# An early-fusion block on one core: small transposes on TensorE, 128-row tiles in the text feed-forward, four row buffers, and another order of gathers

## The chip, the cores and the metric

The kernel runs on one NeuronCore of a Trainium2 chip. The metric is the device time of one launch in microseconds (us); smaller is better. The engines are named as in the profile: PE is TensorE (PEld its weight loads), DVE is VectorE, ACT is ScalarE, POOL is GpSimd, SP is SyncE, which issues most DMAs.

## The reference, cut to what matters

There are 32 samples, each of 36 image patches and 77 text tokens, width 256; with a class token a sample has S = 114 rows. All is float32.

```python
h = patches @ tok_W + tok_b                      # 36 rows, with the class token in front
x = layer_norm(emb[tokens] + pos_emb)            # 77 rows
Q, K, V = x @ Wq + bq, x @ Wk + bk, x @ Wv + bv  # 16 heads of 64
logits = Q @ K.T / 8 + causal + where(tokens == 0, -1e9, 0)
x = x + layer_norm(softmax(logits) @ V @ Wo + bo)
x = x + gelu(layer_norm(x) @ W1 + b1) @ W2 + b2  # text feed-forward, 1024 hidden
h = concatenate([h, x], axis=1)                  # 114 rows
h = h + gated_delta_net(layernorm(h))            # convolution, recurrence over the rows, gate
h = h + experts(layernorm(h))                    # top 4 of 32, and a shared one
h = h + state_mixer(layernorm(h))                # convolution, softplus step sizes, 16 states
h = h + factorised_mlp(layernorm(h))             # entmax gates
```

## The kernel before, in words

The program is a row of stages. Each builds its instruction streams, one per engine, inside a block; at its end all engines meet at a barrier, and SP clears the stage's semaphores (`Core.stage`) before the next begins. The order in each stream is written out by hand. The class `Chain` makes VectorE wait for its own instruction where the next one reads what it wrote.

`opening` (L114) takes the image patches through their projection (9 tiles of 128 rows, `image_tokens`, L536) and the text through embedding, norm and attention. Its loads all go through SP's queue in the order of the code: the tokens, a second copy of them to DRAM in another order (L192, one element at a time), patch weights and first patches, position and norm rows, more patches, then behind a wait for that copy the token numbers of all samples broadcast to 77 partitions (`keys`, L205), then the weights of queries, keys and values, the value bias laid out one value per partition (L216, one element at a time), the class token, and then the stores of normalised text rows (`store_text`, L184) and image rows. The normalised rows of a text sample lie in one of two buffers, so `affine(2)` (L292) waits until the store of sample 0 has landed. TensorE does three patch tiles, turns sample 0, and so on to patch tile 8, and then the first products of queries and keys (L463). VectorE turns the token numbers into float and into the mask (L350 to L352).

`text_mlp` (L576) works on 2464 text rows in 11 units of two tiles of 112 rows. Per unit TensorE projects the attended rows with `w_o` (L760), turns the normalised rows (L769), multiplies by `w1` (L783, 224 columns moving) and by `w2` (L797, 256 columns moving). All engines first wait for ten loads under one semaphore `mw_in`. The products of unit m + 2 with `w_o` stand behind unit m's with `w1`.

`prepare` (L834, first part of `delta_net`) reads all rows again in 8 groups of 4 samples, normalises them, stores them turned, and computes two gates per head (L945). A group's rows [114, 4, 256] are loaded by one DMA into one of two buffers (L828); the load of group g + 2 waits for the scaling of group g. VectorE's order is statistics of g + 1, scaling of g, reading of the gates of g - 1.

`delta_net` itself, `route` and `experts` follow; none of them is changed. `state_mixer` (L2162) works on the same 8 groups. GpSimd fetches the experts' rows by indirect DMAs, 16 per group, into one of two buffers (`gather`, L2216), and raises the variances to the power -1/2 (`power`). The order is: group 0, then for each n half of group n + 1, `power(n)`, the other half. VectorE adds the fetched rows times their gates to the residual (`add_routed`, L2243), takes statistics and scales (`norm`); `step_sizes` (L2278) reads the projected step sizes, waits for ScalarE's logarithm (`softplus`) and writes the scaled inputs of TensorE's `turn_bc`. In step j it adds and normalises the groups in `AHEAD`: group 2 in step 0, groups 3 and 4 in step 1, group j + 3 afterwards; `result(j)` then adds the step's output.

## Time and profile before

| | us |
|---|---|
| median of 3 runs (lowest, highest) | 3156.9 (3155.66, 3166.07) |
| the profiled execution | 3159.19 |
| its span, first to last instruction | 3157.5 |
| TensorE, VectorE, ScalarE, GpSimd busy | 2447.2, 2088.9, 1247.4, 809.4 |
| mean granted clock of TensorE | 0.877 |

The stages' places in the span can be read from their first and last instructions: the opening ends near 521 us, the text stage runs from 523.9 to about 771, prepare from 773.7 to 864, the delta stage from 865.8 to about 2150, routing and experts to 2571, the state mixer from 2575 to 2951.5, and the last stage to the end. A busy engine in one of them says nothing about another, so each is read alone. The clock is the share of full speed that TensorE was granted: 1.00 is 2.4 GHz, 0.50 is 1.2 GHz.

### The profile page before, as it was taken

The page shows a single profiled execution, that of the slowest core. Times are in us where ns is not written, and L with a number is a line of the kernel's source. Part 1 is how long each engine was busy: PE and PEld are TensorE (multiplying, and loading weights), DVE is VectorE, ACT ScalarE, POOL GpSimd, SP SyncE. Part 2 cuts the span into 40 slices and gives each one's busy share as a digit, 9 for nine tenths or more (in the row PEclk, how much of TensorE's full clock was granted, in tenths as well). Part 3 has the DMA queues.
Part 4 walks back from the last instruction along what each step waited for, and adds up shares of the span by engine and source line. Part 5 has one row for each costly group of instructions (what it writes and reads, how often), then busy time and mean ns, then how long its engine had stood idle before and what let it go on. Part 6 is the DMA issues. An engine that isn't in the chain of part 4 may idle for free. (4 is left out here: it accounts for less than half of the span.)

```text
span 3157.5 us, 53822 instructions
## 1 busy us (share of the span) xinstructions
PE 2447.2 (78%) x19384; PEld 1877.8 (59%) x19384; DVE 2088.9 (66%) x5024; ACT 1247.4 (40%) x2999; POOL 809.4 (26%) x646
## 2 busy tenths in 40 slices
PE   6888886997455888888888888876543756689798
PEld 5666664886444666666667666655332644466554
DVE  4777773332338888888888888875454336687573
ACT  0434342221145666665666666643000213344132
POOL 1111100000113332233222222231287125550110
PEclk9999997998578999999999999988665887889799
DMA  5220001001212221111112211111211762110000
GB/s 138 64 67 12 12 9 52 21 24 29 87 64 51 52 52 46 49 48 49 44 48 49 51 49 48 45 44 29 74 51 24 227 198 56 47 52 10 18 24 24
DMA packets 277730, 168.94 MB, mean 54 GB/s; under 512 B 186303, under 2 KB 253702, under 8 KB 277112
## 3 DMA queue, kind: packets, MB, share of 16 engines
q1 hardware_dynamic: 251333, 140.22, 15.8%
q0 software_dynamic: 26112, 25.03, 3.0%
q8 instruction: 166, 2.72, 0.4%
q14 instruction: 119, 0.97, 0.1%
HBM read 99.17 MB, written 73.45 MB: 55 GB/s over the span
## 5 line engine op out<-in xcount | busy, mean ns | idle before, releaser
L1149 POOL TENSOR_TENSOR qd<-decay,qm 114x456 f32<-114x456 f32 x128 | 143.7, 1145 | 651.2 <-DVE qm L1242 499.2
L1563 PE MATMUL d_ps<-d_xT,w_qkv 128*128 128x228 f32 x1024 | 235.0, 389 | 48.3 <-DVE qmask L1357 28.9
L1563 PEld LDWEIGHTS d_ps<-d_xT,w_qkv 128*128 128x128 f32 x1024 | 215.4, 212 | 79.5 <-issue 42.0
L2216 POOL DMA_INDIRECT s_eo<-rows_y,slots_all x128 | 152.5, 1191 | 148.5 <-POOLq L87 110.5
L1210 DVE TENSOR_TENSOR elim_tmp<-ue 128x30 f32<-128x30 f32 (+14 forms) x480 | 179.3, 374 | 13.8
L463 PE MATMUL t_ps<-xT,w_qk 128*128 128x154 f32 x1024 | 150.9, 300 | 40.4 <-DVE qk L300 31.0
L1212 DVE TENSOR_TENSOR ue<-ue,elim_tmp 128x30 f32<-128x30 f32 (+14 forms) x480 | 170.4, 355 | 16.5
L1284 DVE SCALAR_TENSOR_TENSOR y_v<-raw,taps,y_v 128x228 f32<-128x228 f32 x384 | 161.2, 493 | 14.3 <-ACT y_v L1414 14.2
L463 PEld LDWEIGHTS t_ps<-xT,w_qk 128*128 128x128 f32 x1024 | 136.7, 189 | 52.0 <-DVE qk L300 38.2
L1551 PE MATMUL d_ps<-gl,after 114*114 114x456 f32 x256 | 132.7, 637 | 41.0 <-DVE sz L1297 41.0
L1376 ACT ACTIVATE decay<-d_ps,gates 114x114 f32<-114x114 f32 x512 | 133.4, 371 | 65.4 <-PE d_ps L1551 65.0
L1809 POOL DMA_INDIRECT rows_x<-r_xn,slot x128 | 144.7, 1131 | 51.9 <-issue 51.0
L1284 DVE SCALAR_TENSOR_TENSOR y_qk<-raw,taps,y_qk 128x228 f32<-128x228 f32 x384 | 142.2, 450 | 22.1 <-ACT y_qk L1414 21.7
L1387 ACT ACTIVATE gl<-upto,gates 114x114 f32<-114x114 f32 x512 | 151.5, 414 | 0.0
L1168 POOL TENSOR_SCALAR_AFFINE_SELECT ue<-ue 128x1024 f32<-128x1024 f32 x16 | 88.8, 5552 | 236.8 <-DMA ue<-blocks_n 236.8
L1596 PE MATMUL d_ps<-w_out,oT 128*114 128x256 f32 x512 | 132.0, 416 | 16.4 <-ACT oT L1433 16.4
L1662 PE MATMUL d_ps<-upd,ut 114*50 114x64 f32 (+1 forms) x2048 | 134.7, 231 | 2.8 <-issue 2.2
L1662 PEld LDWEIGHTS d_ps<-upd,ut 114*50 114x50 f32 (+1 forms) x2048 | 130.9, 142 | 3.8 <-issue 3.1
L1596 PEld LDWEIGHTS d_ps<-w_out,oT 128*114 128x114 f32 x512 | 99.3, 197 | 48.2 <-ACT oT L1433 20.6
L1579 PE MATMUL d_ps<-w_z,d_xz 128*114 128x512 f32 x256 | 117.1, 601 | 10.2 <-DVE sz L1273 9.2
L268 POOL TENSOR_TENSOR rstd<-rstd,minus_half 77x1 f32<-77x1 f32 x32 | 23.5, 734 | 387.9 <-DVE rstd L283 387.9
L405 ACT COPY pT<-t_ps 77x462 f32<-77x462 f32 (+1 forms) x96 | 45.0, 498 | 192.4 <-PE t_ps L513 187.9
(337 smaller groups left out, 5656.9 us busy)
## 6 DMA issues: line engine op xcount, KB each, us to landing
rows_x<-zero_row SPq DMA_DIRECT2D x4, 2048.0 KB, 7.8
ue<-blocks_n SPq DMA_DIRECT2D x16, 512.0 KB, 4.7
blocks_u<-ue SPq DMA_DIRECT2D x16, 512.0 KB, 2.7
blocks_v<-on SPq DMA_DIRECT2D x16, 512.0 KB, 2.8
e_x<-rows_x SPq DMA_DIRECT2D x32, 256.0 KB, 4.2
e_gu<-L_ffn_w_gate_up SPq DMA_DIRECT2D x32, 256.0 KB, 4.2
rows_y<-e_y SPq DMA_DIRECT2D x32, 256.0 KB, 3.3
blocks_n<-nt SPq DMA_DIRECT2D x96, 64.0 KB
```

Source lines behind the costliest of these rows:

```text
L463: last = pe.matmul(ps[:, 6 + f % 3 % 2, (t - lo) * P2:(t - lo + 1) * P2], w_qk[:, k, t * 128:(t + 1) * 128], xT[pair % 3][:, k, :], start= ...
L1149: pool.tensor_tensor(qd[p.par][s][:, hs(u), :].rearrange("p (a o b) t -> p a o b t", o=2, b=2)[:, :, o], e[o][:, :, :].rearrange("p (a b) ...
L1210: ch(dve.tensor_tensor(part, ue[:, j, j + 1:].unsqueeze(1).to_broadcast([128, j, BW - 1 - j]), ue[:, 0:j, j:j + 1].to_broadcast([128, j, B ...
L1212: step = dve.tensor_tensor(ue[:, 0:j, j + 1:], ue[:, 0:j, j + 1:], part, ALU.subtract)
L1284: dve.scalar_tensor_tensor(y, raw[:, t, :, k:k + S], taps[:, t, k:k + 1], y, ALU.mult, ALU.add).then_inc(conv_r, 1)
L1376: last = act.activation(e[o][:, m, :], ps[0:S, 4 + o, m * S:(m + 1) * S], ACT.Exp, bias=gates[:, bass.ds(p.sample(s), 1), head:head + 1].r ...
L1387: last = act.activation(gl[o][:, m, :], c.upto[:, :], ACT.Copy, scale=gates[:, bass.ds(p.sample(s), 1), head:head + 1].rearrange("p a h -> ...
L1563: last = pe.matmul(ps[:, f % 2, (t % 2) * W:(t % 2 + 1) * W], w_qkv[:, k, t * 128:(t + 1) * 128], xT[:, k, :], start=(k == 0), stop=(k == ...
L1596: last = pe.matmul(ps[0:S, 6, 0:D], oT[:, k, :], w_out[:, k, :], start=(k == 0), stop=(k == 7))
L1662: last = pe.matmul(ps[rows, XBANK[m], i * DH:(i + 1) * DH], ut[s][:, 8 * g + i, rows], x[s][:, 8 * g + i, :], start=True, stop=True)
L1809: pool.indirect_dma_start(out=rows_x, out_offset=bass.IndirectOffsetOnAxis(ap=slot[g % 3][:, s, k:k + 1], axis=0), in_=xn[g % 3][:, s, :], ...
L2216: pool.indirect_dma_start(out=eo[n % 2][:, s * TOPK + k, :], out_offset=None, in_=rows_y, in_offset=bass.IndirectOffsetOnAxis(ap=slots_all ...
```

## The change

In the opening, the token numbers as floats are transposed by TensorE into [32, 77], copied from PSUM and stored to DRAM in 32 long rows (the DRAM tensor is now float32); the broadcast of all token numbers comes behind the query and key weights. The value bias is loaded as 8 rows of 128 and transposed by TensorE. The class token's store moves behind the image rows. The broadcast token numbers lie in a buffer `kw` that outlives the stage, and the output weights `Wo` are loaded into it once the mask is made. The mask is computed from it without a cast. TensorE's first patch products wait for the patch weights only, and not for the bias.

In the text stage tiles have 128 rows; the last unit has 128 + 32, and a function `tile` gives each tile's own count to products, transposes and DMAs. The loads are in three semaphores: three norm rows; the rest with `w1`; `w2`. TensorE starts without a wait. Rows of a unit come in two DMAs.

Prepare has four row buffers; the small weights are issued between the load of group 0 and those of 1 to 3; VectorE reads the gates of group g - 2.

In the state mixer GpSimd issues whole groups behind each power from group 2 on: gathers 0, half of 1, power 0, other half of 1, all of 2, power 1, 3, power 2, 4, power 3, and then power n, gathers n + 1. The first group has one semaphore per sample and is added sample by sample (`add_first`). `step_sizes` is cut in two; its second part `step_gates` comes behind the adding of the next group. In step 1 the result is added between groups 3 and 4. ScalarE's `softplus(0)` comes ahead of its read of group 1.

```diff
@@ opening, SP
-                with nc.allow_non_contiguous_dma(reason="2464 token numbers, once"):
-                    sp.dma_start(c.tok_flat.rearrange("(b t) -> t b", b=B), dr["tokens"]).then_inc(flat_in, 16)
...
+                sp.dma_start(bv8[:, :], dr["L0_txt_bv"].rearrange("(k p) -> k p", p=128)).then_inc(bv_in, 16)
                 load_patches(1)
                 load_patches(2)
-                sp.wait_ge(flat_in, 16)
-                sp.dma_start(keys[:, :, :].rearrange("p b t -> p (b t)"), c.tok_flat.partition_broadcast(NT)).then_inc(key_in, 16)
-                sp.dma_start(causal[:, :], dr["causal"]).then_inc(key_in, 16)
+                sp.wait_ge(tokT_ready, 1)
+                sp.dma_start(c.tok_flat.rearrange("(b t) -> b t", b=B), tokT[:, :]).then_inc(flat_in, 16)
...
+                sp.wait_ge(flat_in, 16)
+                sp.dma_start(keys[:, :, :].rearrange("p b t -> p (b t)"), c.tok_flat.partition_broadcast(NT)).then_inc(key_in, 16)
+                sp.dma_start(causal[:, :], dr["causal"]).then_inc(key_in, 16)
                 sp.dma_start(w_v[:, :, :], dr["L0_txt_Wv"].rearrange("(k p) n -> p k n", p=128)).then_inc(wv_in, 16)
-                with nc.allow_non_contiguous_dma(reason="1024 bias values, one per partition and head pair"):
-                    sp.dma_start(b_v[:, :], dr["L0_txt_bv"].rearrange("(k p) -> p k", p=128)).then_inc(wv_in, 16)
...
+                    if i == 20:
+                        sp.wait_ge(mask_ready, 1)
+                        sp.dma_start(kw[:, 0:8 * D].rearrange("p (k n) -> p k n", k=8),
+                                     dr["L0_txt_Wo"].rearrange("(k p) n -> p k n", p=128)).then_inc(wo_in, 16)
@@ opening, TensorE
-                pe.wait_ge(imgw_in, 32)
+                pe.wait_ge(selected, 4)
+                pe.wait_ge(tokf_ready, 1)
+                pe.transpose(ps[0:B, 0, 0:NT], tokf[:, :], c.ident[0:NT, 0:NT]).then_inc(small_mm, 1)
+                pe.wait_ge(imgw_in, 16)
+                pe.wait_ge(tokT_ready, 1)
@@ text_mlp
-    TP = 112
+    TP = 128
     U = 2 * TP
-    UNITS = B * NT // U
+    UNITS = -(-B * NT // U)
+
+    def tile(m, u):
+
+        return min(TP, B * NT - m * U - u * TP)
...
-                pe.wait_ge(mw_in, 16 * MW)
                 project(0)
                 project(1)
                 turn(0)
                 for m in range(UNITS):
                     pe.wait_ge(xT_ready, 2 * m + 2)
+                    if m == 0:
+                        pe.wait_ge(m1_in, 16 * M1)
@@ prepare
+    HB = 4
...
                 load(0)
-                load(1)
                 for dst, src in (
...
+                for g in range(1, HB):
+                    load(g)
                 for g in range(GROUPS):
-                    if g + 2 < GROUPS:
+                    if g + HB < GROUPS:
                         sp.wait_ge(gxn_ready, g + 1)
-                        load(g + 2)
+                        load(g + HB)
...
-                    if g >= 1:
-                        gate_read(g - 1)
+                    if g >= 2:
+                        gate_read(g - 2)
@@ state_mixer, GpSimd
-                for n in range(G):
-                    if n + 1 < G:
-                        gather(n + 1, 0, GS // 2)
+                gather(1, 0, GS // 2)
+                power(0)
+                gather(1, GS // 2, GS)
+                gather(2, 0, GS)
+                power(1)
+                gather(3, 0, GS)
+                power(2)
+                gather(4, 0, GS)
+                power(3)
+                for n in range(4, G):
                     power(n)
                     if n + 1 < G:
-                        gather(n + 1, GS // 2, GS)
+                        gather(n + 1, 0, GS)
@@ state_mixer, VectorE
+                def add_first():
+
+                    for s in range(GS):
+                        dve.wait_ge(s_first[s], 16 * TOPK)
+                        for k in range(TOPK):
+                            ch(dve.scalar_tensor_tensor(c.resid[:, 1 + s, :], eo[0][:, s * TOPK + k, :], gates_all[:, s, k:k + 1],
+                                                        c.resid[:, 1 + s, :], ALU.mult, ALU.add))
+                    dve.sem_inc(s_used, 1)
...
-                    for n in AHEAD.get(j, (j + 3,)):
-                        if n < G:
-                            add_routed(n)
-                            norm(n)
+                    ahead = [n for n in AHEAD.get(j, (j + 3,)) if n < G]
+                    for n in ahead[:1]:
+                        add_routed(n)
+                    if j + 1 < G:
+                        step_gates(j + 1)
+                    for n in ahead[:1]:
+                        norm(n)
                     result(j)
+                    for n in ahead[1:]:
+                        add_routed(n)
+                        norm(n)
@@ state_mixer, ScalarE
                 token_read(0)
+                softplus(0)
                 xT_read(1)
                 first_tap(1)
-                softplus(0)
```

## Rows read from the trace of the kernel before

**Rows 1.** Busy time by stretches: us and instructions per engine, TensorE's granted clock, DMA share, GB/s.

```profile
5.00:12.00 7.00, 0.00 (x0) 0.00 (x0) 0.00 (x0) 0.00 (x0) 1.12 (x2) 1.00 0.44 29
...
523.00:538.00 15.00, 0.00 (x0) 0.00 (x0) 0.00 (x0) 0.00 (x0) 0.00 (x0) 0.50 0.84 262
557.00:771.00 214.00, 209.09 (x1032) 183.20 (x1032) 73.93 (x200) 45.79 (x110) 15.50 (x20) 1.00 0.07 21
787.00:856.00 69.00, 38.00 (x192) 36.75 (x192) 23.56 (x98) 8.85 (x10) 7.27 (x6) 0.50 0.27 95
883.00:1500.00 617.00, 494.11 (x4865) 386.33 (x4867) 507.67 (x1120) 369.89 (x968) 188.60 (x105) 0.90 0.18 45
```

**Rows 2.** Opening in order of time: start, us, engine, line, operation, [idle before].

```profile
1.31 0.99 SPq L192 DMA_DIRECT2D tok_flat<-tokens  x1
...
4.56 7.37 SPq L188 DMA_DIRECT2D attended_t<-patches  x1
...
21.90 10.83 PE L536 MATMUL t_ps<-attended_t 128*128 128x256 f32 x36 [21.90 <-DMA attended_t<-L_tok_b]
...
26.05 4.43 SPq L216 DMA_DIRECT2D b_v<-L_txt_bv  x1
...
44.51 0.48 DVE L292 SCALAR_TENSOR_TENSOR x<-xg,rstd,ln_b 77x256 f32<-77x256 f32 x1 [9.47 <-DMA text_x<-x]
...
54.70 4.36 PE L463 MATMUL t_ps<-xT,w_qk 128*128 128x154 f32 x32
```

**Rows 3.** The start of the text stage in order of time.

```profile
538.32 9.45 PE L760 MATMUL m_ps<-w_o,attended_t 128*112 128x256 f32 x32 [18.37 <-DMA b2r<-L_txt_b]
...
547.89 0.69 DVE L676 TENSOR_TENSOR m_ao<-m_ps,b_o 112x512 f32<-112x512 f32 x1 [32.93 <-PE m_ps L760]
...
557.30 6.32 PE L783 MATMUL m_ps<-m_xT,w 128*128 128x224 f32 x32 [1.12 <-ACT m_xT L733]
```

**Rows 4.** One steady unit of the text stage in order of time.

```profile
719.44 6.22 PE L783 MATMUL m_ps<-m_xT,w 128*128 128x224 f32 x32
...
725.50 7.07 PE L760 MATMUL m_ps<-w_o,attended_t 128*112 128x256 f32 x32
...
739.70 6.22 PE L783 MATMUL m_ps<-m_xT,w 128*128 128x224 f32 x32
```

**Rows 5.** Prepare in order of time.

```profile
792.81 1.41 DVE L861 BATCH_NORM_STATS2 g_stats<-g_h 114x6 f32<-114x256 f32 x4 [5.91 <-DMA g_h<-hid]
...
794.67 0.17 DVE L866 TENSOR_SCALAR g_rstd<-g_mv 114x4 f32<-114x4 f32 x1
...
841.38 1.78 PE L935 MATMUL g_ps<-ident,g_xn 114*128 114x114 f32 x8 [4.79 <-DVE g_xn L873]
...
855.80 0.23 DVE L883 TENSOR_TENSOR gates<-g_ps,ab_bias 114x64 f32<-114x64 f32 x1 [2.67 <-PE g_ps L945]
```

**Rows 6.** DMA rate over 771 to 787 us, in 40 equal slices.

```profile
GB/s 148 51 0 0 0 0 0 0 0 56 31 41 123 146 143 143 146 146 150 165 149 156 138 136 138 136 138 116 48 8 0 0 0 0 0 0 0 0 0 0
```

**Rows 7.** State mixer in order of time.

```profile
2597.50 1.13 POOL L2216 DMA_INDIRECT s_eo<-rows_y,slots_all  x1 [0.30 <-issue]
...
2601.38 6.80 DVE L2243 SCALAR_TENSOR_TENSOR resid<-s_eo,gates_all,resid 114x256 f32<-114x256 f32 x16 [30.36 <-DMA s_eo<-rows_y,slots_all]
...
2611.29 1.05 POOL L2222 TENSOR_TENSOR s_rstd<-s_rstd,minus_half 114x4 f32<-114x4 f32 x1
...
2684.07 0.17 DVE L2288 TENSOR_TENSOR s_dpos<-s_dpos,s_dsoft 114x4 f32<-114x4 f32 x1 [2.00 <-ACT s_dsoft L2386]
...
2752.26 6.86 DVE L2243 SCALAR_TENSOR_TENSOR resid<-s_eo,gates_all,resid 114x256 f32<-114x256 f32 x16 [12.64 <-DMA s_eo<-rows_y,slots_all]
...
2765.24 1.85 PE L2487 MATMUL s_ps<-s_bcT 16*114 16x114 f32 x8 [9.80 <-DVE resid L2310]
...
2789.82 6.79 DVE L2243 SCALAR_TENSOR_TENSOR resid<-s_eo,gates_all,resid 114x256 f32<-114x256 f32 x16
...
2860.90 6.79 DVE L2243 SCALAR_TENSOR_TENSOR resid<-s_eo,gates_all,resid 114x256 f32<-114x256 f32 x16
```

146 lines of the change are left out of this document (87 added, 59 removed).

## Prediction

> **What bounds the kernel now.** The kernel is a row of stages with a barrier between them, so I cut the span first and asked of each stage that the diff touches which wait ends last in it. The chain of waits that ended last lies wholly in the last stage, which the diff leaves alone; it says nothing here. I read, in this order: the busy time by stretches, where three stretches stand out with TensorE idle or half idle [rows 1]; then the instructions in order of time in each touched stage. What to see there:
> - Opening: TensorE does nothing until 21.9 us [rows 2]. From 5 to 12 us the DMA engines are 0.44 busy and move only 29 GB/s [rows 1]: the store of token numbers, one 4-byte element each, holds the queue, and the first patch load takes 7.37 us to issue behind it [rows 2]. Later VectorE waits 9.47 us for the first text row store to land, behind all the weights.
> - Text feed-forward: TensorE waits until 538.3 for ten loads [rows 3]; after that it is full, 209 of 214 us at clock 1.00 [rows 1]. Columns and instructions decide.
> - Prepare: TensorE works 38.0 of 69 us at clock 0.50 [rows 1]. A row load that can only start when its buffer is free ends each group's wait (5.91 us) [rows 5].
> - State mixer: VectorE works nearly without a break, but waits 30.36 us at the start, 12.64 us for the fifth group's gathers and 2.00 us in each step for a logarithm [rows 7].
>
> **The change part by part.** All sums are against the profiled execution (3159.2 us around a span of 3157.5).
>
> *A, opening.* The element store becomes a TensorE transpose (two small instructions, done by 4 us under the loads) and a store of 32 long rows. The queue is then free from about 3 us; before, the loads flowed freely only from about 13: 10 us. The value bias is also read as 8 rows and transposed; its 1024 elements took 4.43 us to issue [rows 2], and like the first ones they held the queue. By count 1024 of them cost 4.2; a part would have passed beside the weights, so I take 3. What is late next is not TensorE's loads (they would let it start near 9 us and finish six patch tiles near 28) but the third text group: its VectorE instruction waits for the first text store, which still stands behind the same 8.4 MB of loads. It ran at 44.51 [rows 2] and should run at 44.5 - 10 - 3 = 31.5. All behind it keeps its order, so the first query product moves from 54.70 to about 41.7: **13 us**. The cast of the mask that falls away (1.4 us) lies beside TensorE. SP now holds the weights of the query behind the wait for TensorE's transpose and the value weights behind the token store's landing; the queue has 4 MB in front of it then, which hides both. If they aren't hidden, 5 us less. Bounds 8 to 16. The output weights' load moved here lies beside attention.
>
> *B, start of the text stage.* Before, all ten loads (3.5 MB) landed by 538.3; TensorE projected for 9.45 us, VectorE's chain ran from 547.89 and the first hidden product began at 557.30: 9.4 us from chain to product [rows 3]. Now the output weights are there already, so TensorE projects during the loads, and VectorE waits for b_o, the gains, the rows, b2 and w1: 1.8 MB. At the 262 GB/s of this stretch [rows 1] the 1.7 MB less are 6.5 us by bytes; what is left still has the broadcasts, so I take 5: chain from 533.5, product at 543. **14 us**, bounds 11 (second projection late because the clock is low) to 16.
>
> *C, steady text.* A unit of 224 rows takes 739.70 - 719.44 = 20.26 us [rows 4]: the products with 256 columns take 7.07 each whatever the rows, the hidden product 6.22 for 224 columns. With 256 rows the hidden product becomes 7.07 too, so a unit is 21.1. Nine full periods at 20.26 become eight at 21.1: 182.3 - 168.8 = **13.5 us**. The last two units end alike: the last but one waits for VectorE's norm, and the last one's 160 columns lie between 4.4 and 6.2 us, held by its weight loads; I take 6.2. Bounds 12.5 to 15. VectorE's work per unit is the same number of instructions.
>
> *D, prepare.* Two buffers become four and the small weights are issued ahead of the second load. Before: group 2's statistics wait 5.91 us, and so on for each group, and TensorE stands 4.79 before a turn; the last gate read is at 855.80 [rows 5]. After: loads run ahead, and TensorE's 38.0 us [rows 1] (4.75 per group) follow each other from 787, with about 2 of waiting after the first turn: end at 827 against 855.8. **29 us.** VectorE is busy 23.6 us there, 2.9 per group (statistics end 2.03 after they begin [rows 5]), under TensorE. Moving the gate reads one group later takes away a wait and adds none, since the bank is needed only two groups on. Now the DMA: while the first two loads flow, the rate stands at 138 to 165 GB/s [rows 6]; 0.47 MB at 145 are 3.2 us. The store of the same size takes 1.5 at 262/0.84 = 312 GB/s [rows 1]. One after the other that is 4.7 per group, as much as TensorE's, so the sum stands. The Trainium skill ("DMA: Bandwidth & Descriptors", the section on why a DMA increments its semaphore by 16) says that a DMA runs on the largest number of engines up to 16 that divides its outer dimension; for 114 partitions that is 6. The trace agrees in kind: 145 is 0.46 of 312. By that rule no number of buffers makes a load faster, and a higher TensorE clock would bring nothing here; its own estimate of load and store is the same 29 within a microsecond. Bounds of D: 20 (stores land late behind queued loads, 6 per group) to 35 (the clock rises, the last load lands near 813 and 7 us of work follow).
>
> *E, state mixer.* (1) The first group is added sample by sample; that spares VectorE some 4.7 us of adding after the last gather lands at 2601.38. But its power still stands behind 8 further gathers and ran at 2611.29 [rows 7] when the queue reached it: gain 0 to 0.6. (2) The second power now stands behind 24 gathers of 1.43 (1.13 + 0.30), from 2612.5 to 2648 or 2649, where 16 stood; it is asked for near 2644. That makes the second turn 4.5 us later. Against it the softplus goes ahead of the second turn's read, which had kept VectorE waiting; then the next products on TensorE are in place at the same time. Net 0, bounds -5 to +3. (3) The wait of 2.00 for the logarithm [rows 7] is covered by the adding: 2 us in each of the first two steps. (4) Group 4's gathers start behind the third power, near 2693, and land near 2720, long before they are wanted; the wait of 12.64 goes, and with the result placed ahead of group 4 so does TensorE's 9.80 [rows 7]. VectorE would be some 18 us ahead. (5) But from group 5 on the gathers of a group start only behind the power before. VectorE was free for group 4 at 2752.26 - 12.64 = 2739.6; less 3.6 gained by then, plus 1.3 for the result placed ahead it is 2737.4 now, and the statistics end 6.9 + 2.0 later, at 2746.4. Group 5's adding can't start before 2746.4 + 1.3 (power) + 22.9 (16 gathers) + 2.8 (last issue's end to adding, 2601.38 - 2598.63) = 2773.5 to 2774, against 2789.82: 15.7 ahead. From there a group takes 22.9 + 2.8 + 1.3 + 6.9 (adding) + 0.6 + 2.0 (statistics) + 0.4 = 37.0, against (2860.90 - 2789.82)/2 = 35.5: two groups give back 3, and the step sizes now stand behind the adding (0.6). **12 us** are left. Bounds 0 to 19.
>
> *F.* Eleven more semaphores are cleared at stage ends by SP. No row shows a clear; above it lies SP's cheapest kind of entry here, an issue of 0.99 [rows 2], below it 0. A clear moves no data: I take 0.6 us in all, near the lower end.
>
> Sum: 13 + 14 + 13.5 + 29 + 12 - 0.6 = 80.9. 3159.2 - 80.9 = 3078.3. The profiled execution is 2.3 above the median of the runs (3156.9), so 3076.
>
> **Rivals.**
> 1. *GpSimd's queue becomes the mixer's bound at once.* If a gather slows down beside VectorE or the second power's 4.5 us carry through, E is 0: 3088. For it: (5) already has the pool as the bound. Against: the wait of 12.64 is plainly gone.
> 2. *Prepare stays with its transfers.* Loads sit ahead of stores in one queue, ScalarE's copy waits for the store two groups back. If load, store and the store's landing (some 1.7 of the 5.91) follow each other, a group takes 3.2 + 1.5 + 1.7 = 6.4: 7 x 1.65 = 11.6 lost, 3088. Against: two groups' buffers lie between.
> 3. *The change doesn't do what it says in the opening:* the text store's wait stays at 44.5, since the broadcast of keys and the weights are what it waits for. A is 3 (the bias alone): 3086. Against: the loads can't flow before 12 us in the row of before, and can afterwards.
> 4. *Slower: TensorE's clock in the delta stage.* That stage is untouched, but runs at a mean granted clock of 0.90 with TensorE 494 of 617 us busy [rows 1], so stretches of it are at 1.2 GHz. Should the shifted start put more of it there, the whole stage of 1267 us has some 1040 of TensorE: at 0.90 to 0.83 that is 1040 x (0.90/0.83 - 1) = 88 us, which eats the 81: 3164. It decides from a mean of 0.835 down. Against: the stage starts behind a barrier and its own loads in both kernels, with TensorE at 0.50.
>
> **How the numbers follow.** About 9 us (0.3%) is what a measurement of this kernel can tell. The forecast, each term within its bounds: 0.66, 3076. Rivals 1, 2, 3, singly or two together, 3086 to 3101: 0.25. Better than all terms (the DMA or the clock helps): 0.05. Rival 4 and other losses of this size 0.04, of which 0.02 end within 0.3% and 0.02 slower. All lower bounds together save 51, the best ones 98, so the range is 3058 to 3106. Faster 0.96, same 0.02, slower 0.02.
>
> **What would show it.** A: first patch product near 9 us, the third group's affine near 31.5, first query product near 42. B: TensorE at work from the stage's first microsecond, first hidden product 10 us after the rows and w1 are there. C: ten periods of 21.1. D: groups 4.7 apart at the turn, no wait on the row loads after the third. E: no wait for group 4's gathers, but waits of some us for those of 5, 6 and 7, and groups 37 apart. The prediction is wrong if the delta stage's length changes by more than 5 us, or if one of the groups in D or E has a period that isn't TensorE's or GpSimd's.

## The result, and the profile after

The changed kernel takes 3083.1 us (median of 4 runs, 3074.2 to 3086.1) against 3159.4 for the kernel before (4 runs on the same chip, 3155.7 to 3166.1). The ratio is 0.9755, 95% interval 0.9733 to 0.9776: 2.4% faster. The forecast was 3076 us in a range of 3058 to 3106. The profiled execution's span is 3083.9 us against 3157.5, which is 73.6 less where the sum of the steps said 80.9.

The first view of the changed kernel is the busy time by stretches: the opening's loads, the text start, steady text, prepare, and 617 us of the delta stage that begin, as in [rows 1], 16.5 us after its first row load (columns: us, then PE, PEld, DVE, ACT, POOL, granted clock, DMA share, GB/s).

```profile
5.00:12.00 7.00, 3.09 (x7) 2.52 (x8) 0.81 (x2) 0.00 (x0) 1.10 (x2) 1.00 1.06 311
520.00:536.00 16.00, 11.10 (x45) 8.93 (x43) 7.43 (x20) 0.18 (x1) 1.59 (x2) 0.89 0.44 157
536.00:741.00 205.00, 196.13 (x932) 169.21 (x932) 66.86 (x181) 44.82 (x101) 13.93 (x18) 0.99 0.08 22
753.00:792.00 39.00, 36.76 (x192) 36.30 (x192) 23.40 (x98) 8.84 (x10) 8.06 (x7) 0.50 0.44 156
819.80:1436.80 617.00, 495.95 (x4856) 387.00 (x4857) 505.64 (x1114) 369.14 (x968) 182.02 (x104) 0.89 0.18 45
```

From 5 to 12 us the DMA engines now move 311 GB/s where they moved 29. In prepare TensorE is busy 36.76 of 39 us where it was 38.00 of 69. The delta stage looks as before: TensorE is busy 495.95 of the 617 us (494.11 before), at a granted clock of 0.89 (0.90).

The opening of the changed kernel in order of time:

```profile
8.91 11.06 PE L548 MATMUL t_ps<-attended_t 128*128 128x256 f32 x36 [5.40 <-DMA attended_t<-patches]
...
19.72 0.31 SPq L217 DMA_DIRECT2D key_tok<-tok_flat  x1
20.08 0.35 SPq L218 DMA_DIRECT2D causal_sb<-causal  x1
20.48 0.40 SPq L219 DMA_DIRECT2D w_v<-L_txt_Wv  x1
20.92 0.87 SPq L188 DMA_DIRECT2D text_x<-x  x2
...
34.16 0.48 DVE L300 SCALAR_TENSOR_TENSOR x<-xg,rstd,ln_b 77x256 f32<-77x256 f32 x1 [12.16 <-DMA text_x<-x]
...
45.22 4.47 PE L475 MATMUL t_ps<-xT,w_qk 128*128 128x154 f32 x32
```

The first patch product is 13.0 us earlier than in [rows 2], the third text group only 10.4, the first query product 9.5. VectorE's wait for the text store has grown from 9.47 to 12.16 us. Two more rows of the kernel before belong beside this:

```profile
30.52 9.19 SPq L218 DMA_DIRECT2D hid<-L_tok_cls_token  x1
39.76 0.93 SPq L184 DMA_DIRECT2D text_x<-x  x2
```

Before, SP took 9.19 us to issue the class token's store and issued the text store only at 39.76, and 4.7 us later VectorE went on. Now the text store is issued 18.8 us earlier, at 20.92, but VectorE goes on only 13.2 us after that. So 8.5 of the 18.8 us are lost in the landing.

The start of the text stage, whose first DMA is issued at 512.48:

```profile
512.53 9.28 PE L789 MATMUL m_ps<-key_tok,attended_t 128*128 128x256 f32 x32 [4.48 <-PEq L87]
...
525.67 0.69 DVE L704 TENSOR_TENSOR m_ao<-m_ps,b_o 128x512 f32<-128x512 f32 x1 [22.82 <-DMA w<-L_txt_W]
...
526.41 8.86 PE L789 MATMUL m_ps<-key_tok,attended_t 128*128 128x256 f32 x32 [4.61 <-DVE m_ao L704]
...
536.89 7.17 PE L815 MATMUL m_ps<-m_xT,w 128*128 128x256 f32 x32 [1.18 <-ACT m_xT L762]
```

TensorE works from the first microsecond, but VectorE then waits for W1, and the second projection takes 8.86 us where a warm one takes 7.07 [rows 4].

Prepare in the changed kernel: VectorE's statistics of the second, third and fourth group, then TensorE's turns of groups 3 and 4 and the gate products between.

```profile
750.20 1.40 DVE L898 BATCH_NORM_STATS2 g_stats<-g_h 114x6 f32<-114x256 f32 x4 [3.10 <-DMA g_h<-hid]
...
753.60 1.41 DVE L898 BATCH_NORM_STATS2 g_stats<-g_h 114x6 f32<-114x256 f32 x4
...
757.75 1.41 DVE L898 BATCH_NORM_STATS2 g_stats<-g_h 114x6 f32<-114x256 f32 x4 [0.84 <-DMA g_h<-hid]
```

```profile
761.51 1.76 PE L973 MATMUL g_ps<-ident,g_xn 114*128 114x114 f32 x8
763.07 3.16 PE L983 MATMUL g_ps<-w_ab,g_xT 128*114 128x32 f32 x16
766.04 1.76 PE L973 MATMUL g_ps<-ident,g_xn 114*128 114x114 f32 x8
```

No row on TensorE shows idle time between turn and gates. The turns stand 4.53 us apart (766.04 - 761.51), at a granted clock of 0.50, which is the 1.2 GHz level, although the engine is full for 35 us.

The mixer in the changed kernel, whose first gather starts at 2508.86 (before: 2575.87): the last two samples of the first group, then the groups 5, 6 and 7.

```profile
2528.38 2.04 DVE L2302 SCALAR_TENSOR_TENSOR resid<-s_eo,gates_all,resid 114x256 f32<-114x256 f32 x4 [3.57 <-DMA s_eo<-rows_y,slots_all]
2534.55 2.05 DVE L2302 SCALAR_TENSOR_TENSOR resid<-s_eo,gates_all,resid 114x256 f32<-114x256 f32 x4 [4.12 <-DMA s_eo<-rows_y,slots_all]
...
2704.39 6.80 DVE L2291 SCALAR_TENSOR_TENSOR resid<-s_eo,gates_all,resid 114x256 f32<-114x256 f32 x16 [3.86 <-DMA s_eo<-rows_y,slots_all]
...
2741.77 6.80 DVE L2291 SCALAR_TENSOR_TENSOR resid<-s_eo,gates_all,resid 114x256 f32<-114x256 f32 x16 [3.07 <-DMA s_eo<-rows_y,slots_all]
...
2779.43 6.80 DVE L2291 SCALAR_TENSOR_TENSOR resid<-s_eo,gates_all,resid 114x256 f32<-114x256 f32 x16 [5.02 <-DMA s_eo<-rows_y,slots_all]
```

The wait of 12.64 us [rows 7] is gone and three waits of 3 to 5 us have come, with periods of 37.4 and 37.7 us.

### The profile page after: what moved, and what is told of

Same layout as the page of the kernel before. It is cut to its first block and busy times, and to the rows that moved or that the text cites. A ratio compares the mean times of both kernels' runs of the same rounds, so it can differ in the third digit from the quotient of the medians.

```text
span 3083.9 us, 53608 instructions
## 1 busy us (share of the span) xinstructions
PE 2436.0 (79%) x19286; PEld 1864.6 (60%) x19286; DVE 2084.8 (68%) x5004; ACT 1244.2 (40%) x2990; POOL 815.8 (26%) x644
## 5 line engine op out<-in xcount | busy, mean ns | idle before, releaser
L1248 DVE TENSOR_TENSOR elim_tmp<-ue 128x30 f32<-128x30 f32 (+14 forms) x480 | 178.8, 372 | 13.8
L1250 DVE TENSOR_TENSOR ue<-ue,elim_tmp 128x30 f32<-128x30 f32 (+14 forms) x480 | 171.9, 358 | 16.5
L1206 POOL TENSOR_SCALAR_AFFINE_SELECT ue<-ue 128x1024 f32<-128x1024 f32 x16 | 98.6, 6162 | 238.1 <-DMA ue<-blocks_n 238.1
```

Source lines behind the costliest of these rows:

```text
L1248: ch(dve.tensor_tensor(part, ue[:, j, j + 1:].unsqueeze(1).to_broadcast([128, j, BW - 1 - j]), ue[:, 0:j, j:j + 1].to_broadcast([128, j, B ...
L1250: step = dve.tensor_tensor(ue[:, 0:j, j + 1:], ue[:, 0:j, j + 1:], part, ALU.subtract)
```

## Experiments

Twelve kernels ran. Since barriers part the stages, each run is read by landmarks of its profile, and the time of the whole is only the second witness. The start of the last instruction is taken where a column ends with one, and some landmarks were read to one decimal, so that an entry can be 0.1 off. The columns of this table (us, from the trace of each kernel's profiled run): q, the first query product; att, from there to the last ScalarE instruction of the opening; start, the text stage's first DMA to its first hidden product; text, from there to the last result; prep, prepare's first DMA to the delta stage's first row load; delta+, from there to the mixer's first gather; mix, from there to the last stage's first VectorE instruction; last, from there to the end; and the median time.

```
            q     att   start  text   prep  delta+   mix    last   median
before     54.7  465.9  33.4  211.1   92.8  1709.4  378.0  203.6   3159.4
after      45.2  463.5  24.4  197.3   63.8  1705.7  366.2  208.8   3083.1
b_open     43.5  463.7  32.4  211.1   92.5  1713.0  375.8  209.4   3153.2
b_text     55.4  463.6  26.2  197.3   93.0  1712.8  375.6  203.0   3135.2
b_prep     56.3  467.6  33.0  211.1   63.3  1715.3  372.0  209.5   3129.9
b_mix      58.4  463.4  33.5  211.1   93.0  1716.6  365.2  209.5   3155.1
a_wv       41.7  463.2  23.9  197.3   64.1  1705.6  366.3  208.9   3080.8
a_chain    44.1  459.4  19.0  197.2   63.8  1704.3  366.2  209.0   3076.3
a_half     44.2  468.9  23.8  197.2   63.7  1705.0  348.6  209.5   3069.9
a_soft     44.4  467.7  23.9  197.3   63.8  1706.0  373.1  209.0   3092.0
a_hb2      43.4  463.2  23.8  197.3   91.5  1705.5  365.9  209.3   3110.9
a_cut      43.4  459.3  24.0  197.2   61.3  1698.5  366.2  209.1   3080.0
a_x1       36.3  461.8  24.0  197.3   63.2  1709.9  366.0  209.0   3075.1
all_four   36.0  463.5  18.8  197.3   61.1  1699.8  351.4  203.6   3043.1
```

b_ is the kernel before with one part of the change; a_ is the changed kernel with one edit. Medians of different groups come from different chips, on which the kernel before took 3160.4 (b_), 3166.8 (a_wv to a_soft), 3162.3 (a_hb2 to a_x1) and 3161.8 (all_four); ratios below are to these. The medians alone can't tell most single edits from the changed kernel: its ratio is 0.9755 (0.9733 to 0.9776), that of a_wv 0.9727 (0.9670 to 0.9785), a_chain 0.9722 (0.9663 to 0.9781), a_x1 0.9715 (0.9686 to 0.9744), a_half 0.9687 (0.9629 to 0.9746) and a_soft 0.9759 (0.9697 to 0.9822). What these edits are worth is read from the landmarks of one profile each.

### One part of the change at a time

**b_open**: the opening alone.

```diff
 # before.py, opening() and program() of after.py, without
-                    if i == 20:
-                        sp.wait_ge(mask_ready, 1)
-                        sp.dma_start(kw[:, 0:8 * D]..., dr["L0_txt_Wo"]...)
 # the text stage loads w_o itself, as before
```

> The kernel before with the opening of the changed kernel alone (tokens and value bias turned by TensorE, new order of SyncE's queue; the output weights stay a load of the text stage). In the changed kernel the first query product moved from 54.70 to 45.22 (9.5 us) and the opening's last ScalarE instruction from 520.96 to 509.06 (11.9). Theory (the parts are independent, since barriers part the stages): first query product at 45.2, end of the opening at 509 to 510, all later stages as in the kernel before; total 3159.4 - 11.5 = 3148 us. Rival (the shift of the start puts the delta stage at another clock, so parts do not add up): the delta stage's length differs from before's 1710.0 us (first DMA of it to the mixer's first gather) by more than 5 us, total off 3148 by as much.

Measured: first query product at 43.5, opening's end 507.5, text, prepare and mixer within 2.2 us of before. The ratio to before is 0.9975 (0.9958 to 0.9991), so 7 to 8 us gained where 11.5 were expected; the interval, 3 to 13 us, holds both. In the profile its last stage took 209.4, and 203.6 in the profile of before. The delta part is 3.6 longer, within the 5 us.

**b_text**: the 128-row tiles and split counters alone. The lines are those by which its text stage differs from the changed kernel's.

```diff
+        w_o = sb("w_o", [128, 8, D])
...
+                    (w_o[:, :, :], dr["L0_txt_Wo"]...),   # first load of the stage, counted in mn_in
                     (b_o[:, :], dr["L0_txt_bo"].partition_broadcast(TP)),
...
+                pe.wait_ge(mn_in, 64)
                 project(0)
```

> The kernel before with the 128-row text tiles and their split counters alone; the output weights are still loaded at the start of the text stage, ahead of everything, and TensorE waits for them. Theory: the steady part gains what the changed kernel shows, 13.8 us (first hidden product to last result 197.3 against 211.1), and of the start (9.0 us gained in the changed kernel) only little, since TensorE's projections again stand behind 1 MB: first hidden product between before's 33.4 us and the changed kernel's 24.4 us after the stage's first DMA, about 28. Total 3159.4 - 13.8 - 5 = 3140 to 3146. Rival: the start is set by W1's landing alone, wherever the output weights stand: first hidden product 24 to 25 us after the first DMA, total 3137. Rival 2: the gain of the steady part is not the tile's but the new order of loads: then 13.8 does not show.

Measured: 197.3 us of steady text, equal to the changed kernel, and 26.2 for the start. The time is 3135.2, ratio 0.9918 (0.9886 to 0.9949), 5 us below the range that was expected. Its start in order of time shows why it loses so little although TensorE waits for 1 MB more:

```profile
529.39 9.46 PE L772 MATMUL m_ps<-w_o,attended_t 128*128 128x256 f32 x32 [11.06 <-DMA ln_b<-L_txt_ln_b]
539.74 7.17 PE L772 MATMUL m_ps<-w_o,attended_t 128*128 128x256 f32 x32 [0.89 <-DVE m_ao L687]
```

The second projection follows the first within 0.89 us and takes 7.17, not 8.86. So 7.2 of the start's 9.0 us come with the new order and the counters, and the output weights' load in the opening adds only 1.8, as long as VectorE's chain waits for W1 (a_chain below). The first rival (24 to 25) isn't met, the second is out.

**b_prep**: prepare alone (the function of the changed kernel in the kernel before).

> The kernel before with the four row buffers, small weights ahead of the second load and gate reads one group later in prepare alone. Theory (independent part): turns 4.53 us apart with TensorE without a gap at clock 0.50, from the stage's first DMA to the last gate read 52.6 us against 82.1, total 3159.4 - 29.5 = 3130. Rival (it also moves the delta stage's clock): delta stage's length off 1710 by more than 5 us.

Measured: stage 63.3 against 92.8, median 3129.9, ratio 0.9892 (0.9873 to 0.9912): 29.5 gained, as expected. The delta part took 1715.3, 5.9 more than in the profile of before. The rival's bound of 5 is passed. But in b_mix, where all code ahead of the mixer is that of the kernel before, the same part takes 1716.6, 7.2 more than in the profile of before. So a difference of this size comes without any edit, and the bound of 5 us was too narrow to tell.

**b_mix**: the state mixer alone (the function of the changed kernel in the kernel before).

> The kernel before with the state mixer of the changed kernel alone (first group added sample by sample, gathers behind each power, softplus ahead, result ahead of the second of two groups). Theory: from the first gather to the last result 363.3 us against before's 375.6, total 3159.4 - 12.3 = 3147, with waits of 3 to 5 us for the gathers of groups 5, 6 and 7. And the last stage follows the mixer at another moment of TensorE's clock: in the changed kernel it took 208.8 us (from its first VectorE instruction to the end) against 203.6; if that comes from the mixer's new ending, it shows here too (total 3152); if it is chance, it does not.

Measured: 365.2 us against 378.0 in the profile of before, with waits of 5.74, 3.11 and 4.94 for groups 5 to 7. So the mixer gives 12.8 us. The median is 3155.1, ratio 0.9976 (0.9959 to 0.9993), a gain of 2 to 13 us, where 3147 or 3152 was expected. Its last stage took 209.5. But b_open and b_prep, whose mixer is the old one, show 209.4 and 209.5 too, and b_text 203.0: the last stage takes 203 or 209 whatever the mixer is. The theory that the mixer's ending sets it falls.

### The steps of the forecast that were off

**a_wv**: the value weights issued behind the text stores.

```diff
-                sp.dma_start(w_v[:, :, :], dr["L0_txt_Wv"]...).then_inc(wv_in, 16)
                 store_text(0)
                 store_text(1)
+                sp.dma_start(w_v[:, :, :], dr["L0_txt_Wv"]...).then_inc(wv_in, 16)
```

> The changed kernel with one line moved: the value weights (1 MB) are issued behind the first two text row stores instead of ahead of them. In the changed kernel the store is issued at 20.92 and VectorE's third text group waits 12.16 us for it, to 34.16; before the change the same store landed within 4.7 us of its issue. Theory (the change put the value weights, delayed by the wait for the token store, right ahead of the text store in the one queue, and that took back 3 of the 13 us I had forecast for the opening): the third group's instruction comes at 27 to 29, TensorE's 6.60 us before the third turn fall to under 1, first query product at 38.6 to 41 against 45.22, opening 4 to 6 us shorter. Rival (the store waits for the two query and key weight loads issued from 10.08 on, which stay ahead of it): third group at 33 to 34, first query product at 44 to 45, no gain.

Measured: between the theory and the rival. The third group comes at 31.18 and the first query product at 41.7:

```profile
31.18 0.48 DVE L300 SCALAR_TENSOR_TENSOR x<-xg,rstd,ln_b 77x256 f32<-77x256 f32 x1 [9.26 <-DMA text_x<-x]
```

The store, issued at 19.97, still needs until 31. The query and key weights, which the rival names, are not what it waits for last: in this run the last of their four loads was issued at 13.87 and landed 12.9 us later, at 26.8. Right ahead of the store stand the token numbers for 77 partitions (741 KB, issued at 19.21) and the causal rows. In a_x1 below, VectorE's mask waits for these two, issued at 18.95 and 19.31, until 31.30. In the changed kernel the value weights stand behind them, land at 33.7 (20.48 + 13.2), and the store's wait ends at 34.16. So with the value weights out of the way the store comes when the token numbers do; their place was moved by the change too. No run moves the token numbers alone, so this part of the cause is read from landings and not from an edit. The Trainium skill (DMA: Bandwidth & Descriptors, Queues, rings and completion order) says that a DMA's semaphore increment lands only after every earlier write from the same DMA engine. The two runs agree in kind: the wait for the store ends 13.2 us after its issue with token numbers and value weights ahead, and 11.2 with the token numbers alone.

**a_x1**: four row buffers, so that the wait for the store goes away for the third and fourth group.

```diff
+        NX = 4
+        x1 = [sb(f"x1_{k}", [NT, D]) for k in range(NX)]
...
-                    if i >= 2:
-                        dve.wait_ge(x1_out[i % 2], 16 * (i // 2))
-                        dve.wait_ge(x1_t, i - 1)
+                    if i >= NX:
+                        dve.wait_ge(x1_out[i % NX], 16 * (i // NX))
+                        dve.wait_ge(x1_t, i - NX + 1)
```

> The changed kernel with four instead of two row buffers in the opening's text part, so that the third and fourth group no longer wait for a store to land (the value weights stay ahead of the stores). With the value weights moved behind the stores the third group came at 31.18 instead of 34.16 and the first query product at 41.7 instead of 45.2: half of what I had expected of it, since the store still landed 11 us after its issue, behind the query and key weights. Theory: the third group comes at 22, TensorE has no 6.60 us of idle before the third turn, first query product at 37.5 to 39, opening 6 us shorter. Rival (the key numbers or weights land later than 30 us and hold VectorE's mask or TensorE's first query product): first query product at 41 to 43, another wait in front of it.

Measured: third group at 22.43, first query product at 36.3, better than the 37.5 to 39 expected. What is late next is the mask, and the wait before TensorE's small product there is only 0.98 us:

```profile
22.43 0.48 DVE L302 SCALAR_TENSOR_TENSOR x<-xg,rstd,ln_b 77x256 f32<-77x256 f32 x1 [0.54 <-POOL rstd L278]
...
31.30 1.44 DVE L363 TENSOR_SCALAR mask<-key_tok 77x2464 f32<-77x2464 f32 x1 [5.13 <-DMA causal_sb<-causal]
```

```profile
35.97 0.19 PE L573 MATMUL t_ps<-ident,b_v 8*128 8x8 f32 x1 [0.98 <-DVE attended_t L336]
```

**a_chain**: VectorE's first unit no longer waits for W1.

```diff
                 dve.wait_ge(mn_in, 48)
-                dve.wait_ge(m1_in, 16 * M1)
...
                     dve.wait_ge(x3_ready, m + 1)
+                    if m == 0:
+                        dve.wait_ge(m1_in, 16 * M1)
                     ch(dve.tensor_tensor(x2[m % 2]..., b2...))
```

> The changed kernel, but VectorE starts the first text unit once the output bias, the norm's vectors and the rows are there, and waits for b2 and W1 only at the last addition of the unit (TensorE waits for W1 itself). In the changed kernel the chain starts 13.2 us after the stage's first DMA and the first hidden product 24.4. Theory (the wait for W1 in front of the chain is what I missed in the forecast of the start): chain at 9.4 to 10 us, but then the second projection (8.86 us, held until the first result is read) is late next on TensorE and ends 3.8 us earlier than now: first hidden product 20.5 to 21 us after the first DMA, 3.8 us gained. Rival (the rows or vectors land as late as W1): chain at 13, nothing gained. Rival 2 (W1's own landing is late next): first hidden product not before 22, gain 2.

Measured: 19.0 us for the start, 5.4 less than 24.4, where 3.8 were expected. The rows, with the stage's first DMA at 507.26:

```profile
516.73 0.69 DVE L704 TENSOR_TENSOR m_ao<-m_ps,b_o 128x512 f32<-128x512 f32 x1 [19.07 <-PE m_ps L790]
```

```profile
517.47 7.17 PE L790 MATMUL m_ps<-key_tok,attended_t 128*128 128x256 f32 x32 [0.86 <-DVE m_ao L704]
```

The chain starts 9.5 us after the first DMA, as soon as the projection ends. The extra 1.7 us are the second projection: without the 4.61 us pause it runs in 7.17 instead of 8.86.

**a_half**: half of the next group's gathers ahead of the power from group 4 on.

```diff
                 for n in range(4, G):
+                    if n + 1 < G:
+                        gather(n + 1, 0, GS // 2)
                     power(n)
                     if n + 1 < G:
-                        gather(n + 1, 0, GS)
+                        gather(n + 1, GS // 2, GS)
```

> The changed kernel, but from group 4 on half of the next group's gathers (8) stand ahead of the power and half behind it, as before the change. In the changed kernel VectorE waits 3.86, 3.07 and 5.02 us for the gathers of groups 5, 6 and 7, which start only behind the power of the group before; periods of 37.4 and 37.7 us. Theory (the change moved the mixer's bound to GpSimd's order, not its load: its 16 gathers take 22.9 of 37 us): the three waits go, periods fall to 34 to 35, the mixer takes 354 to 357 us against 366.2, total 10 to 12 us less. Rival (the power itself becomes late behind 8 gathers): new waits of 1 to 5 us for the power in each group, mixer 360 or more. Rival 2 (TensorE or ScalarE is right behind): VectorE waits elsewhere, mixer 362 to 366.

Measured: 348.6 us against 366.2, and the median 3069.9, ratio to before 0.9687 (0.9629 to 0.9746). The additions of groups 5, 6 and 7 have no wait left and stand 32.7 apart, better than the expected 34 to 35 (mixer 354 to 357):

```profile
2702.19 6.85 DVE L2293 SCALAR_TENSOR_TENSOR resid<-s_eo,gates_all,resid 114x256 f32<-114x256 f32 x16
...
2734.91 6.80 DVE L2293 SCALAR_TENSOR_TENSOR resid<-s_eo,gates_all,resid 114x256 f32<-114x256 f32 x16
...
2767.53 6.80 DVE L2293 SCALAR_TENSOR_TENSOR resid<-s_eo,gates_all,resid 114x256 f32<-114x256 f32 x16
```

The power is not late behind 8 gathers: VectorE's normalisation waits 1.24 us for it in each of these groups, as long as in the changed kernel. The gain of 17.6 is more than the three waits (11.95). The rest shows in VectorE's waits for TensorE. In the changed kernel it also waits before each late reading of the step sizes:

```profile
2699.93 0.29 DVE L2340 TENSOR_SCALAR s_ssm<-s_ps 114x132 f32<-114x132 f32 x1 [2.44 <-PE s_ps L2536]
...
2738.10 0.29 DVE L2340 TENSOR_SCALAR s_ssm<-s_ps 114x132 f32<-114x132 f32 x1 [1.87 <-PE s_ps L2536]
...
2812.99 0.29 DVE L2340 TENSOR_SCALAR s_ssm<-s_ps 114x132 f32<-114x132 f32 x1 [2.06 <-PE s_ps L2536]
```

None of these waits (6.4 us together) is left in a_half, while one wait in the last result grows by 1.4. TensorE's granted clock from group 4's addition to group 7's is 0.97 instead of 0.91. So the edit gives back more than the waits for the gathers.

**a_soft**: the first softplus back behind the next group's taps.

```diff
-                softplus(0)
                 xT_read(1)
                 first_tap(1)
+                softplus(0)
```

> The changed kernel with the first softplus of the state mixer put back behind the second group's turn read and first taps on ScalarE. My forecast had put the second power's lateness (4.5 us, measured 4.0) and this edit at net 0; measured, the second group's taps came 4.5 us EARLIER against the stage's first gather than before the change. Theory (the softplus ahead is worth the difference, 8.5 us: VectorE's gates no longer wait for ScalarE's taps of the next group, which ended 15 us of idling): the second group's taps come about 8 us later than in the changed kernel, the mixer takes 372 to 375 against 366.2. Rival (the gain is swallowed by GpSimd's order later, since from group 5 on the gathers set the pace): taps later by 8, but the mixer's whole only 0 to 3 us longer.

Measured: the mixer takes 373.1 against 366.2, as the theory says, and the wait is back in one row:

```profile
2602.51 0.16 DVE L2347 TENSOR_TENSOR s_dpos<-s_dpos,s_dsoft 114x4 f32<-114x4 f32 x1 [15.29 <-ACT s_dsoft L2452]
```

Against its first gather's time the second group's taps begin 8.2 us later (2603.11 - 2512.2 = 90.9; changed kernel 2591.56 - 2508.86 = 82.7), and 6.9 of it reach the end. Median 3092.0.

**a_hb2**: two row buffers in prepare.

```diff
-    HB = 4
+    HB = 2
```

> The changed kernel with two row buffers in prepare instead of four; the small weights stay ahead of the second load and the gate reads one group later. Theory (the buffers are the gain: with two, a load can start only when VectorE has scaled the group two back, and 3.2 to 4 us of load end each wait): turns about 9 us apart again as before the change (its loads are issued 9.0 us apart), prepare's stage 92 to 93 us against 63.8, total 3083 + 29 = 3112. Rival (half of the gain is the gate read's move, which took a wait on TensorE's gate products out of VectorE's order between two groups): period 6 to 7 us, stage 73 to 79.

Measured: 91.5 us and a period of 8.9, median 3110.9, ratio to before 0.9834 (0.9807 to 0.9860). TensorE waits before each turn again:

```profile
768.86 1.78 PE L973 MATMUL g_ps<-ident,g_xn 114*128 114x114 f32 x8 [4.17 <-DVE g_xn L910]
770.43 3.16 PE L983 MATMUL g_ps<-w_ab,g_xT 128*114 128x32 f32 x16
777.78 1.78 PE L973 MATMUL g_ps<-ident,g_xn 114*128 114x114 f32 x8 [4.19 <-DVE g_xn L910]
```

So the step from two to four buffers is worth 27.7 of the 29 us, and 1.3 are left for the order of the small loads and the gate read.

**a_cut**: the row loads of prepare cut at partition 112.

```diff
-                    sp.dma_start(hs[g % HB][:, :, :], hid[...]...).then_inc(h_in[g % HB], 16)
+                    rows = hid[g * GS:(g + 1) * GS].rearrange("b s d -> s b d")
+                    sp.dma_start(hs[g % HB][0:112, :, :], rows[0:112]).then_inc(h_in[g % HB], 16)
+                    sp.dma_start(hs[g % HB][112:S, :, :], rows[112:S]).then_inc(h_in[g % HB], 16)
```

> The changed kernel with each row load of prepare cut into partitions 0 to 111 and 112 to 113. In the changed kernel the first load lands 5.67 us after its issue; the first two loads flow at 119 to 146 GB/s, half of what the stores reach. The Trainium skill (DMA: Bandwidth & Descriptors) says that a DMA takes the largest number of engines up to 16 that divides its outer dimension: 6 for 114, 16 for 112. By that rule the first load lands some 1.5 us earlier and the rate while loads flow doubles. Theory: TensorE sets the period (4.53 us, without a gap), so only the start is shortened: stage 62 us against 63.8, turns still 4.53 apart, total 2 us less. Rival (the rate is set by the 1 KB elements): landing after 5.5 to 6 us, rate unchanged, stage 63.8 to 64.5.

Measured: the stage takes 61.3 us, 2.5 less, and the turns still follow every 4.53. The median, 3080.0, can't tell 2.5 from none, since that kernel's runs lie between 3069.8 and 3085.9. The DMA rate over 735 to 800 us in 40 slices, first of the changed kernel (first load issued at 739.41), then of this one (issued at 733.0):

```profile
GB/s 74 27 0 42 152 116 29 144 144 138 138 139 127 153 292 145 315 134 200 259 140 251 206 142 299 75 0 287 0 40 247 5 123 164 0 0 0 0 0 0
```

```profile
GB/s 196 27 216 264 238 122 32 248 160 253 338 265 142 250 261 63 287 0 49 248 0 131 156 0 218 75 0 286 1 0 0 0 0 0 0 5 43 289 320 408
```

While its second, third and fourth load flow (slices 8 to 13 of the first line) the rate is 127 to 144; with the cut the same loads flow at 216 to 264 (slices 3 to 5 of the second line). The first load lands after 3.9 us instead of 5.67. By the rule that the Trainium skill states (DMA: Bandwidth & Descriptors, on why a DMA increments its semaphore by 16), 114 rows go to 6 engines and 112 to 16. The runs agree in kind and not in size: the mean of the slices named rises from 138 to 239 GB/s, 1.7 times. No view here shows how many engines a load used.

### All together

**all_four**: the edits of a_x1, a_chain, a_cut and a_half in one kernel.

```diff
+ a_x1 (NX = 4)   + a_chain (m1_in later)   + a_cut (0:112, 112:S)   + a_half (gathers around the power)
```

> The changed kernel with the four edits together: four row buffers in the opening, VectorE's text chain ahead of the wait for W1, cut row loads in prepare, and gathers of the mixer around the power from group 4 on. Each alone, by its stage's landmarks: first query product 36.3 against 43.4 to 45.2 (8), first hidden product 5 us sooner after the stage's start, prepare 61.3 against 63.8 (2.5), mixer 348.6 against 366.2 (17.6). Theory (the parts are independent, barriers between them): all four landmarks again within 1 us, total 3083 - 33 = 3050, range 3043 to 3057 for the scatter of the untouched delta stage (1698 to 1717 in the runs so far). Rival (an earlier stage's gain comes back as time at the lower clock in the delta or last stage): delta to experts over 1717 or last stage over 210, total above 3057.

Measured: 3043.1 us (3041.0 to 3045.7, 5 runs), ratio to the kernel before 0.9626 (0.9607 to 0.9646), against 0.9755 for the change alone. Three of the four landmarks fall within 0.3 us of their single runs (36.0, 18.8, 61.1); the mixer's 351.4 is 2.8 above a_half's and misses the expected 1 us. From group 4's addition on, its TensorE ran at a granted clock of 0.93 and then 0.96, where a_half had 0.97 and 0.98. The rival is out: the delta and last stages took nothing back (1699.8 and 203.6). They gave 5.9 and 5.3 us against the profile of the changed kernel, so only 32 of the 43 us between the two profiles belong to the four edits.

## Why the prediction was right, step by step

The mechanism held in the steps B to E. In A the wait that binds was right and the path to it was not. The sum of 80.9 was 7.3 too much. The profiles of before and after differ by: q 9.5, att 2.4, start 9.0, text 13.8, prepare with its borders 29.1, delta+ 3.7, mixer 11.8, last stage -5.2; the pause between opening and text took back 0.5. That is 73.6. The stages that the change touches gave 75.1 of it, 5.8 less than the sum, and 5.0 of that is step B. The two untouched parts nearly cancel.

- **A, opening** (forecast 13). The first product came at 8.91, as said. The third group was to come at 31.5 and came at 34.16, and the first query product moved by 9.5 instead of 13. Over all kernels the step is larger: the first query product lies at 54.7 to 58.4 in the four with the old opening (mean 56.2) and at 43.4 to 45.2 in the seven whose opening is the change's (mean 44.0), so 12.2. The sum of 10 and 3 had the wrong path. It let the text store come earlier by what the two element-wise DMAs cost, at an unchanged distance to its landing. In the rows its issue moved by 18.8 us, since the class token's store (9.19 us to issue, in no term of the sum) no longer stands ahead of it, and its landing grew by 8.5. That the difference of 10.4 is near 13 is partly luck. With the value weights issued behind the store, and not 0.4 us ahead of it, the third group comes 3.0 us sooner (a_wv). That the store is what binds was right: a_x1, where nothing waits for it, moves the first query product from that mean of 44.0 to 36.3. Rival 3 (3 us) is out as a time, but what it names, the token numbers' broadcast, lands when the store does in a_wv.
- **B, text start** (forecast 14, measured 9.0). This step failed in size, and below its bound of 11. I took W1 as landed 9.6 us after the stage's start, since 1.7 MB less were to be loaded; VectorE's chain waited until 13.2. The 1 MB that went from the queue's head gives only 1.8 (b_text). And the pause of 4.61 us made the second projection slow (8.86), which I had put in the lower bound only. a_chain gives 5.4 us back by taking that wait away.
- **C, steady text** (forecast 13.5, measured 13.8, and the same 197.2 to 197.3 in every kernel with the new tiles). A unit takes 558.15 - 536.89 = 21.3 at the start and 21.2 on average up to 706.54, so the periods gave 12.7 and not 13.5. The last unit's 160 columns took 4.3, the low end; I had taken 6.2 since weight loads would hold them. From the last but one hidden product on, the end is 1.1 us shorter than before, where the forecast had it alike. The two errors cancel.
- **D, prepare** (forecast 29, measured 29.0; b_prep 29.5, both by the table). TensorE's 4.53 us per group at clock 0.50 set the pace, as forecast. The forecast's transfers of 4.7 us per group would have been as slow, but a_cut shows that they were not the bound: faster loads leave the period alone. Rival 2 (6.4 per group) is out.
- **E, mixer** (forecast 12, measured 11.8, b_mix 12.8 against the same profile). Two parts of it were off and cancelled. The first two steps were to be net 0: the second power was 4.0 us late, as said, but the second group's taps came 4.5 us earlier, since the softplus is worth 8.2 there (a_soft): in the kernel before, VectorE waits 15.09 us for the logarithm in the first step, and the forecast had 2.00 for every step. Later GpSimd's order takes that back: 37.4 and 37.7 us per group where I had 37.0. Group 5's addition was 18.4 us ahead of before (forecast 15.7), group 7's 14.5. Over kernels the step is smaller: mixers of the old kind took 372.0 to 378.0 (mean 375.4), of the new kind 365.2 to 366.3: 9.4. Rival 1 (E is 0) is out. What is true of it stood in step (5) too: GpSimd's order binds from group 5 on, and with half of the gathers ahead of the power the mixer is another 17.6 shorter (a_half; 14.8 in all_four).
- **F** (forecast -0.6): the pause between the opening's last work and the text stage's first DMA grew from 2.95 to 3.4.
- **Rival 4**, the delta stage's clock: out. The part is 3.7 us shorter in the profile of after than in that of before, within the forecast's 5 us, though b_prep and b_mix show that 5 us lies within the scatter. Its start lay between 786 and 868 us in fourteen kernels and its length, with routing and experts, between 1698.5 and 1716.6.
- **The range**: its best bounds add up to 101 less 0.6 and not to 98, so its lower end should have been 3056.5. Nothing hangs on it.

What no step held is the scatter of stages that the change leaves alone. The last stage takes 203 or 209 us. Between 40 and 80 us after its first VectorE instruction the granted clock is 0.96 in the three profiles with 203 (before, b_text, all_four) and 0.83 in all eleven with 209; 40 us times the difference of 0.13 is 5.2, which is what the stage lost from before to after. What decides between the two isn't settled. Delta+ gave 3.7 of it back. Nor is why delta+ took 1709 to 1717 in the five kernels built on the one before and 1698 to 1710 in the nine built on the changed one, a mean difference of 9 us that no single part brings.

## What to carry to other kernels

When a queue is unblocked, read what now stands ahead of the next store in it: here a store that frees a buffer landed 11 to 13 us after its issue, with the loads issued just before it, and four buffers for two took it off the path. When a stage's start is sped up by moving one load away, list each engine's first wait anew; a wait for a group of loads is as late as its last member, even if the engine needs that one much later. When an in-order queue serves two purposes (gathers ahead, a power now), all of one behind the other can make a new bound; here half and half hid both.

## What the runs showed of the hardware

- TensorE stayed at the 1.2 GHz level through prepare (granted clock 0.50) although the rows leave no gap from 757 to 792 us. All its instructions there have 114 or 32 columns; that this is the reason is not shown.
- After a pause of 4.61 us between two projections the second took 8.86 us, at a mean granted clock of 0.83 from 526 to 536; after pauses of 0.86 and 0.89 (a_chain, b_text) it took 7.17.
- 32 products over 160 columns took 4.34 us from their start to the next product's (722.60 to 726.94), over 256 columns 6.91 (558.15 to 565.06): by columns 4.32, so the weight loads did not hold it.
- Row loads over 114 partitions moved 127 to 144 GB/s, the same rows cut at 112 moved 216 to 264.
- SP took 9.19 us to issue the class token's store right behind the element-wise load of the value bias (4.43 us) in the kernel before, and 0.68 us at its new place behind the image rows.
- A wait for a 77 KB store ended 11.2 us after its issue behind 741 KB of token numbers (a_wv), and 13.2 us after it with 1 MB of value weights between (after).
